# Performer features of a fused token model: one folded product against keys and queries first, then block-diagonal features

## The reference, cut to what matters

```python
def softmax_kernel_features(data, proj, is_query):
    data_normalizer = 1.0 / math.sqrt(math.sqrt(d))
    ratio = 1.0 / math.sqrt(proj.shape[0])
    data_dash = jnp.einsum('bhnd,md->bhnm', data_normalizer * data, proj)
    diag_data = jnp.sum(jnp.square(data), axis=-1, keepdims=True) * 0.5 * data_normalizer * data_normalizer
    if is_query:
        stab = jnp.max(data_dash, axis=-1, keepdims=True)
    else:
        stab = jnp.max(data_dash)
    return ratio * (jnp.exp(data_dash - diag_data - stab) + EPS)
q1 = softmax_kernel_features(q, proj_mat, is_query=True)
k1 = softmax_kernel_features(k, proj_mat, is_query=False)
kv = jnp.einsum('bhnm,bhnd->bhmd', k1, v)
z = 1.0 / jnp.einsum('bhnm,bhm->bhn', q1, jnp.sum(k1, axis=2))
out = jnp.einsum('bhnm,bhmd->bhnd', q1, kv) * z[..., None]
```

## Time and profile before

| | us |
|---|---|
| median of 3 runs | 4841.63 |
| lowest, highest | 4832.39, 4851.4 |
| the profiled execution's own time | 4837.13 |
| its span | 4835.4 |
| token stage | 0 to 88.7 |
| Performer, keys | 88.7 to 404.2 |
| Performer, queries | 404.2 to 787.9 |

### The profile page before, as it was taken

One profiled execution on the slowest core, in us unless ns is written; L12 is line 12 of the kernel. 1 busy time (PEld: TensorE's weight loads), 2 busy tenths in 40 slices (PEclk: granted clock), 3 DMA queues, 4 the chain that ended last, 5 costly groups with the idle time before them and its releaser, 6 DMA issues. The chain is left out here.

```text
span 4835.4 us, 139337 instructions
## 1 busy us (share of the span) xinstructions
PE 4659.4 (96%) x57372; PEld 3846.6 (80%) x57372; DVE 2454.3 (51%) x7361; ACT 2200.9 (46%) x5115; POOL 1532.3 (32%) x2383
## 2 busy tenths in 40 slices
PE   5999998999979999999999999999999999899999
PEld 3666775666658888888888888888888888799998
DVE  4665554566545555554555555455545545352333
ACT  2443442455545555544544554455455545212444
POOL 1000001566653333333333333333333333000555
PEclk8999997899989999999999999999999999899999
DMA  4112110000000000000000000000000000242333
GB/s 99 26 22 50 36 36 6 1 2 1 1 12 2 13 3 13 13 2 13 13 13 2 13 13 8 7 13 13 2 13 13 13 2 13 60 100 68 63 65 57
DMA packets 123765, 110.63 MB, mean 23 GB/s; under 512 B 65385, under 2 KB 111806, under 8 KB 123142
## 3 DMA queue, kind: packets, MB, share of 16 engines
q1 hardware_dynamic: 95986, 66.76, 5.9%
q0 software_dynamic: 16528, 23.16, 2.7%
q10 hardware_dynamic: 10628, 11.80, 1.1%
HBM read 59.76 MB, written 41.48 MB: 21 GB/s over the span
## 5 line engine op out<-in xcount | busy, mean ns | idle before, releaser
L2098 PE MATMUL PS<-th_kT,th_qg 64*125 64x274 f32 x10560 | 1416.9, 400 | 0.0
L1816 POOL TENSOR_TENSOR th_qg<-th_qT,w_th_th 128x180 f32<-128x180 f32 x1760 | 846.3, 503 | 1636.0 <-PE PS L2098 1625.0
L2004 ACT ACTIVATE th_P<-PS 110x600 f32<-110x600 f32 x880 | 647.2, 735 | 1117.1 <-PE PS L2085 1117.1
L1923 DVE TENSOR_REDUCE th_nmx<-PS 125x1 f32<-125x548 f32 x880 | 641.1, 729 | 902.2 <-PE PS L2098 902.2
L2085 PEld LDWEIGHTS PS<-th_mixn,th_P 61*110 61x110 f32 x17600 | 980.4, 173 | 103.4 <-issue 25.5
L2098 PEld LDWEIGHTS PS<-th_kT,th_qg 64*125 64x125 f32 x10560 | 938.8, 184 | 142.0 <-issue 0.2
L2085 PE MATMUL PS<-th_mixn,th_P 61*110 61x60 f32 x17600 | 976.2, 254 | 1.8 <-ACT th_P L2004 1.8
L2014 ACT ACTIVATE th_P<-PS,th_nb 125x548 f32<-125x548 f32 x880 | 621.4, 706 | 106.9 <-DVE th_nb L1926 106.9
L1289 POOL TENSOR_SCALAR ga_P<-ga_P,ga_rw 110x110 f32<-110x110 f32 (+4 forms) x240 | 264.9, 1115 | 207.0 <-DVE ga_rw L1455 207.0
L2120 PEld LDWEIGHTS PS<-th_P,th_v 110*32 110x32 f32 x11520 | 246.7, 116 | 31.0 <-issue 29.9
L2120 PE MATMUL PS<-th_P,th_v 110*32 110x90 f32 (+1 forms) x11520 | 268.0, 254 | 3.3 <-issue 2.4
(11 more groups left out here) (341 smaller groups left out, 6327.8 us busy)
## 6 DMA issues: line engine op xcount, KB each, us to landing
pf_xT<-pf_spill SPq DMA_DIRECT2D x32, 412.5 KB, 5.5
ex_tokens<-th_xn SPq DMA_DIRECT2D x128, 82.5 KB
pf_spill<-pf_xT SPq DMA_DIRECT2D x16, 412.5 KB, 3.7
ex_turned<-th_rT SPq DMA_DIRECT2D x16, 412.5 KB, 3.1
ez_x<-ex_turned SPq DMA_DIRECT2D x32, 206.2 KB
out_h<-X SPq DMA_DIRECT2D x16, 330.0 KB
ex_w<-in_L_ffn_W ACTq DMA_DIRECT2D x18, 288.0 KB
ex_w<-in_L_ffn_W ACTq DMA_DIRECT2D x8, 576.0 KB
```

Of the source, the lines that this page charges most:

```text
L1816: ins = pool.tensor_tensor(qg[:, m % SB, :, 64 * s:64 * s + HQ].rearrange("p c (h n) -> p c h n", n=QH), qT[:, im % 2, :, at + s * QH:at + ...
L1923: dve.tensor_reduce(nmx[:, p:p + 1], PS[0:MR, bank:bank + 2, 0:HK], AX.XY, ALU.max, negate=True) \
L2004: act.activation(P2[:, :, :, at * QT:(at + 1) * QT].rearrange("p t h (s n) -> p s (t h) n", s=2), PS[0:R, MB:MB + 2, 0:VO].rearrange("p s ...
L2098: ins = pe.matmul(PS[0:MR, bank + a, 0:HK], qg[s, p, c, 0:MR], kT[s, im % 2, c, :], start=c == 0, stop=c == NC - 1)
```

## The change

The folded weights go. TensorE first makes keys and queries themselves with channels on partitions: the weights are now the stationary operand and the token block streams (110 columns). Keys are in two blocks of 128 columns of `pf.wK` on array rows 0 to 63, values in three matmuls on rows 64 to 127; queries are one pair of blocks, three chunks each. ScalarE copies the result, scaled, to `kT` in SBUF and squares that into `sq`. From `kT` come the features, by products with a block-diagonal matrix `pf.feat` (four heads, 176 columns, on 64 rows, a pair; and two heads, 88 columns, on 32 rows at partitions 0 and 96, a pair), and from `sq` the sums of squares, by the same four tiles with `pf.sums` (4 and 2 columns), into columns 490 to 495 of the same banks. VectorE reads the sums there. The orders of ScalarE and TensorE in a step change as shown; VectorE's order of whole parts stays. The transposes L459, the products L469 and their copies in `patch_tokens` are gone; `pf.feat` is loaded in eight transfers, key, query and value weights in seven in place of four.

```diff
-    pf.wK = sb(pf_ctx, "pf_wK", [128, NC, HM + D])
-    pf.wQ = sb(pf_ctx, "pf_wQ", [128, NC, HM + C])
+    pf.wK = sb(pf_ctx, "pf_wK", [128, NC, 256])
+    pf.wQ = sb(pf_ctx, "pf_wQ", [128, NC, 128])
+    pf.feat = sb(pf_ctx, "pf_feat", [128, HQ4 * M])
+    pf.sums = sb(pf_ctx, "pf_sums", [128, HQ4])
...
-                sp.dma_start(wqk[:], chunked(A["L0_attn_W_qkv"])[:, :, 0:2 * D]).then_inc(wqk_in, 16)
...
-                for h in range(HC):
-                    sp.dma_start(feat[h * HD:(h + 1) * HD, h * M:(h + 1) * M], A["attn_proj_matT"]).then_inc(feat_in, 16)
...
+                for h in range(2 * HQ4):
+                    sp.dma_start(pf.feat[h * HD:(h + 1) * HD, h % HQ4 * M:(h % HQ4 + 1) * M], A["attn_proj_matT"]).then_inc(pf_in, 16)
                 for a in range(2):
...
+                    sp.dma_start(pf.wK[0:PC, :, a * PIECE:(a + 1) * PIECE], pieces[:, :, D + a * C:D + a * C + PIECE]).then_inc(pf_in, 16)
+                    sp.dma_start(pf.wQ[0:PC, :, a * PIECE:(a + 1) * PIECE], pieces[:, :, a * C:a * C + PIECE]).then_inc(pf_in, 16)
+                sp.dma_start(pf.wK[0:PC, :, 128:256], pieces[:, :, D + PIECE:2 * D]).then_inc(pf_in, 16)
+                sp.dma_start(pf.wK[PC:128, :, 0:D], pieces[:, :, 2 * D:3 * D]).then_inc(pf_in, 16)
+                sp.dma_start(pf.wQ[PC:128, :, 0:128], pieces[:, :, PIECE:D]).then_inc(pf_in, 16)
...
                 def peak(u):
                     p = KB0 + 2 * (u % 2)
-                    dve.wait_ge(ksq, u + 1)
+                    dve.wait_ge(kdash, u + 1)
+                    dve.tensor_copy(diag[:, u, :].rearrange("p (a h) -> p a h", a=2), PS[0:R, p:p + 2, DG:DG + HC]).then_inc(kdiag, 1)
...
-                    dve.tensor_reduce(diag[:, u, :], sq[:, u % 4, :].rearrange("p (h d) -> p h d", d=HD), AX.X, ALU.add) \
-                       .then_inc(kdiag, 1)
...
                 def features(u):
...
-                    dve.wait_ge(qsq, u + 1)
+                    dve.wait_ge(qdash, u + 1)
                     dve.tensor_reduce(mq[:, u % 2, :].rearrange("p (a h) -> p a h", a=2), dash, AX.X, ALU.max).then_inc(qmax, 1)
-                    dve.tensor_reduce(dq[:, u % 2, :], sq[:, u % 4, :].rearrange("p (h d) -> p h d", d=HD), AX.X, ALU.add) \
-                       .then_inc(qdiag, 1)
...
+                    dve.tensor_tensor(dq[:, u % 2, :].rearrange("p (a h) -> p a h", a=2), PS[0:R, p:p + 2, DG:DG + HC],
+                                      mq[:, u % 2, :].rearrange("p (a h) -> p a h", a=2), ALU.add).then_inc(qadd, 1)
...
                 def keys(u):
                     p = KB0 + 2 * (u % 2)
                     act.wait_ge(kprod, u + 1)
+                    act.activation(kT[:, u % 2, :], PS[:, p, KT:KT + 2 * R], ACT.Copy, scale=-0.5).then_inc(kT_in, 1)
...
+                    act.wait_ge(kT_in, u + 1)
+                    act.activation(sq[:, u % 2, :], kT[:, u % 2, :], ACT.Square, scale=HALF).then_inc(ksq, 1)
...
                     if u0 < NT:
                         keys(u0)
+                        take(u0 + 2)
+                        keys(u1)
+                        take(u1 + 2)
                         raise_keys(u0)
-                        keys(u1)
-                        take(u0 + 2)
-                        take(u1 + 2)
                         raise_keys(u1)
...
+                def queries(u):
                     p = QB0 + 2 * (u % 2)
                     act.wait_ge(qprod, u + 1)
...
+                    act.activation(kT[:, u % 2].rearrange("p (a n) -> p a n", a=2), PS[:, p:p + 2, KT:KT + R], ACT.Copy, scale=0.5) \
+                       .then_inc(qT_in, 1)
+
+                def square(u):
+                    act.wait_ge(qT_in, u + 1)
+                    act.activation(sq[:, u % 2, :], kT[:, u % 2, :], ACT.Square, scale=HALF).then_inc(qsq, 1)
...
+                    def key(i, c):
+                        return pe.matmul(PS[:, p, KT + i * R:KT + (i + 1) * R], wK[0:PC, c, i * 128:(i + 1) * 128], xT[0:PC, slot(u), c, cols(u)],
+                                         start=c == 0, stop=c == NC - 1)
+
+                    def value(c):
+                        pe.matmul(PS[0:R, p + 1, HM:HM + D], xT[PC:128, slot(u), c, cols(u)], wK[PC:128, c, 0:D],
+                                  start=c == 0, stop=c == NC - 1)
+
+                    key(0, 0)
+                    value(0)
+                    key(0, 1)
+                    key(0, 2)
+                    value(1)
+                    key(1, 0)
+                    key(1, 1)
+                    value(2)
+                    key(1, 2).then_inc(kprod, 1)
+
+                def dashes(p, u):
+                    for a in range(2):
+                        s = slice(a * PIECE, (a + 1) * PIECE)
+                        pe.matmul(PS[0:R, p + a, 0:HQ4 * M], kT[s, u % 2, 0:R], feat[s, :], start=True, stop=True)
+                    for a in range(2):
+                        s = slice(a * 96, a * 96 + 32)
+                        ins = pe.matmul(PS[0:R, p + a, HQ4 * M:HM], kT[s, u % 2, R:2 * R], feat[s, a * 2 * M:(a + 1) * 2 * M],
+                                        start=True, stop=True)
+                    return ins
+
+                def squares(p, u):
+                    for a in range(2):
+                        s = slice(a * PIECE, (a + 1) * PIECE)
+                        pe.matmul(PS[0:R, p + a, DG:DG + HQ4], sq[s, u % 2, 0:R], sums[s, :], start=True, stop=True)
+                    for a in range(2):
+                        s = slice(a * 96, a * 96 + 32)
+                        ins = pe.matmul(PS[0:R, p + a, DG + HQ4:DG + HC], sq[s, u % 2, R:2 * R], sums[s, 2 * a:2 * a + 2],
+                                        start=True, stop=True)
+                    return ins
+
+                def key_features(u):
+                    if u < NT:
+                        p = KB0 + 2 * (u % 2)
+                        pe.wait_ge(kT_in, u + 1)
+                        pe.wait_ge(v_in, u + 1)
+                        dashes(p, u)
+                        pe.wait_ge(ksq, u + 1)
+                        squares(p, u).then_inc(kdash, 1)
...
                         keys(u0)
+                        turn(u0 + 2)
                         keys(u1)
-                        turn(u0 + 2)
                         turn(u1 + 2)
+                        key_features(u0)
                     gather(u0 - LAG)
+                    if u1 < NT:
+                        key_features(u1)
                     gather(u1 - LAG)
...
-                            ins = pe.matmul(PS[0:R, p + a, 0:HM + C], xT[half, qslot(u), c, cols(u)], wQ[half, c, :],
+                            ins = pe.matmul(PS[:, p + a, KT:KT + R], wQ[half, c, :], xT[half, qslot(u), c, cols(u)],
...
+                def query_features(u):
+                    p = QB0 + 2 * (u % 2)
+                    pe.wait_ge(qT_in, u + 1)
+                    dashes(p, u)
+                    pe.wait_ge(qsq, u + 1)
+                    squares(p, u).then_inc(qdash, 1)
...
                     turn_outputs(a - 4)
                     turn_features(a - 2)
+                    if a < NT:
+                        query_features(a)
                     numerators(b - 4)
                     project(a - 4)
+                    if a < NT:
+                        query_features(b)
                     turn_features(b - 2)
                     turn_outputs(b - 4)
                     numerators(a - 2)
```

More of the change, by code:

```diff
@@ L577, in performer @@
     W34, VW = 2 * HV, 4 * HV
+    feat, sums = k.pf.feat, k.pf.sums
     wK, wQ, wp, own34, epsrow, eps = k.pf.wK, k.pf.wQ, k.pf.wp, k.pf.own34, k.pf.epsrow, k.pf.eps
@@ L948, in keys @@
                         pe.wait_ge(kexp, u - 1)
-                    for c in range(NC):
-                        for a in range(2):
-                            half = slice(a * PC, (a + 1) * PC)
-                            ins = pe.matmul(PS[0:R, p + a, 0:HM + D], xT[half, slot(u), c, cols(u)], wK[half, c, :],
-                                            start=c == 0, stop=c == NC - 1)
-                    ins.then_inc(kprod, 1)
+                    if u >= 2:
+                        pe.wait_ge(kdiag, u - 1)
```

76 lines of the change are left out of this document (22 added, 54 removed).

## The result

The changed kernel takes 5422.03 us (median of 4 runs, 5399.73 to 5479.58) against 4839.65 us: a ratio of 1.1219, 95% interval 1.112 to 1.1318. The profiled execution took 5401.51 us, its span is 5399.8 us.

A forecast was written before the change was run, and what follows sets the result against it. TensorE's own order of work was taken to bound both stages: 4837 + 58 (keys) + 116 (queries) + 4 (token stage) = 5015 us, plus 178 for lost clock = 5193, rounded to 5190 us; range 4950 to 5350.

The forecast's parts named there:

- The key step at the full clock: Key stage, 2.4 GHz: step of 8.8 us against 7.37, with 14 tiling changes; +58 us in 40 steps.
- 24 pair passes of 0.385: Key step: the old key products removed, counted as 24 pair passes of 0.385 us.
- Keys and values run beside each other: Key step: 12 value passes of 0.16 us run beside the key passes; otherwise 1.9 us a step more, +77 us.
- The wait in the query step: Query step: TensorE's turn of outputs waits for divide(b-4) and add(a-4), queued behind features(b): a new 2.2 us.
- The query step at the full clock: Query stage, 2.4 GHz: step of 12.3 us in place of 9.41, or +116 us in 40 steps.
- Token stage: Token stage: more SyncE weight issues ahead of the text make L302 begin some 3.6 us later; +4 us (0 to +5).
- The query stage's clock: Query stage: three quarters of the steps at 1.2 GHz, 16.6 us each; 30 x 4.3 us added.
- The key stage's clock: Key stage: a quarter of the steps at 1.2 GHz, 13.7 us each; 10 x 4.9 us added.
- the spacing of L1581: Passes of 3 columns spaced 0.098 us; basis for estimating that weight-load-bound passes stay as long at 1.2 GHz.
- Rival 2: Key and query stages: the whole Performer falls to 1.2 GHz, 368 us over 5015, 5383 us; chance 0.08.

The follow-up runs named there:

- the last run: Kernel before, with 24 pair passes of 4 columns ahead of the products of every second query tile, results overwritten: 4978.9 us, 1.0313.
- two kernels with the same key code: Changed kernel with bursts ahead of both stages, VectorE's order mended and 64-row pairs: 5046.4 us; the same with ScalarE's order mended too: executions 5124.02, 5107.75, 4878.28, 5120.54 us.

## Why the prediction was wrong, point by point

The direction was right, and so were the costs at the full clock and the wait; the time lay 72 us above the range. What failed is the clock of the key stage, both how many steps it takes in and what a step costs at 1.2 GHz. Against the profiled execution (5401.5 us, forecast 5190):

- **The key step at the full clock**: 8.8 us forecast, 8.9 measured (the run with a burst inside the stage). So close a match is in part luck: a features group up to the gather is 1.41 us, as forecast (0.90 + 0.36 + 0.15 for the change to the gather), but three changes between 64 and 32 rows cost 0.44 us where I had 0.36, and the passes some 0.08 less than my 0.90. The mean change is then 0.15 us, as between 64 and 110 rows, not 0.12. The Trainium skill, TensorEngine Tiling (Array Packing), Key Properties, has any change of tiling mode drain the engine; the runs with 64-row pairs agree, 0.44 us for three changes. (The "24 pair passes of 0.385" of the forecast are 12 pair passes, which show as 24 rows; the sum used 4.62 us and is not touched by it.)
- **Keys and values run beside each other**, as taken: the key passes come every 0.213 us at 1.2 GHz whether a pass of the values goes with them or not.
- **The wait in the query step**: 2.2 us forecast in front of the turn of the outputs, 1.95 (1.4 in the slower steps) measured, with `add(a-4)` as releaser, and it went with VectorE's order. The query step at the full clock follows from the 13.66 us at 0.88 (an estimate): 0.24 of it at 1.2 GHz, of which half is lost, leaves 12.0 against 12.3.
- **Token stage**: +4 us forecast, +0.9 measured. The text transfers of L302 began 2.9 us later (21.37 against 18.47) and held SyncE for 45.5 us in place of 46.7.
- **The query stage's clock**: 129 us forecast for it, 617.1 - (383.7 + 116) = 117 measured. This is luck as well: I had three quarters of the steps wholly at 1.2 GHz and a quarter wholly at 2.4; the trace has 17.0 us at 0.60 in the first half and 13.66 at 0.88 in the second, and the two runs with bursts and nothing else needed 674 and 688 us, bursts included.
- **The key stage's clock**: here the sum failed, in two terms. I let a quarter of the key steps run at 1.2 GHz; it was all of them but the last. And I put the step at 13.7 us there; it is 15.93. The clock cost 642.2 - (306.1 + 58) = 278 us where I had 49. These 229 us are more than the whole miss; about 147 are the 30 steps more (30 x 4.9), the rest the price of a step.

The second of these terms is a plain mistake of price. I took passes bound by their weight load as independent of the clock, by the spacing of L1581, and no row of 1.2 GHz stood behind it. In the changed kernel a key pass with 128 weight columns comes every 0.213 us at 1.2 GHz, one of the gather every 0.150, the second pair pass of 4 columns 0.207 behind the first; at 2.4 GHz, in the run with a burst inside the stage, the same three are 0.112, 0.079 and 0.117. All nearly double. The 24 key passes alone are 5.1 us a step in place of 4.4, the 24 of the gather 3.6 in place of 2.6.

For the first term, I read the falls of the clock as short, since in the kernel before it always came back. In the changed kernel it stayed down from the first key product to the last key step, and a burst of wide products lifted it for two steps only. That the doubling of every pass, short ones too, is what keeps it down is an argument, not shown by a run. Rival 2, the whole Performer at 1.2 GHz, had 0.08 and was right for the keys. That its 5383 us lie so near is a coincidence: it had the key step 2.2 us too cheap and the queries wholly at 1.2 GHz, where their clock was 0.72.

What made the clock fall is settled as far as this: short passes alone do it, without any idle time (the last run); with 64-row pairs, waits add to it (the clock that came back with ScalarE's order was worth three times the wait); added passes of 192 columns hold it in the keys; and the queries with 64-row pairs and both orders mended hold it for the most part (0.96 and 0.89 over the stage in two traces). The Trainium skill, TensorE: Matmul & The Clock Gate, HAM oscillation, tells of the clock falling where matmuls stop to wait between groups. The runs agree for the query step, where 1.1 us of waiting went together with 3 us of lower clock, and add the case of an engine that does not stop.

**Open**: why one execution of the same code keeps 2.4 GHz in the keys and the next does not (by time, where there is no trace: 1 of 4 with 64-row pairs alone, 3 of 4 and 1 of 4 in two kernels with the same key code, 2 of 4 with bursts and sorted 32-row pairs, but 10 of 10 with the keys grouped); why the changed kernel's query step went from 17.0 to 13.66 us at 1053 us; and how rows in work and changes of rows share the effect of the 32-row pairs. One thing to look at for the keys: the clock also came up in the changed kernel's last key step, where, as in the grouped order, no turn stands between the two key groups.

## What to carry to other kernels

A product that is split so that it streams less is not cheaper by the columns it saves: count the passes, the changes of row tiling between them, and ask what is left that streams wide. Here, without that, TensorE's clock went down and stayed down, and then the short passes cost nearly double as well as the wide ones. Before a kernel's structure is judged, mend the order of the engines that drain it: here two edits in the written orders of VectorE and ScalarE were worth nothing and 165 us, the one with 32-row pairs and a clock that stayed down, the other with 64-row pairs and a clock that came up with it. A cheap test of such a stage is to add wide work that is thrown away; where the time falls, as in the keys, the clock is the cause. Where it does not fall, as in the queries with their waits, the test says nothing.

## What the runs showed of the hardware

- Added matmuls made the kernel faster: 1.9 us of passes of 192 columns in each key step (an estimate from their count and 0.16 us each) took the stage from 642 to 451 us.
- The spacing of passes that are bound by their weight load follows the granted clock: 0.112 us at 2.4 GHz and 0.213 at 1.2 for 128 weight columns, 0.079 and 0.150 for 89.
- TensorE's clock falls under a record that is busy without a gap: behind 24 pair passes of 4 columns (2.5 us) it is 0.69 in one stretch of 3 us and 0.74 in the next.
- A change between 64 and 32 rows costs 0.15 us at 2.4 GHz in the mean of three, as one between 64 and 110 does; at 1.2 GHz the same three cost 0.20 each (2.39 against 1.80 us). Padding 32 rows to 64 with zero weights saves it.
- One and the same key code ran its 40 steps at 2.4 GHz in one trace and nearly all of them at 1.2 GHz in another: 336.0 and 591.6 us.
